# Gathers of the experts' results spread over 112 steps of attention instead of 32, with the division of the heads between them

## What is computed

```
xn = layernorm(x)
s = attention(xn)          # 4 batches x 16 heads of width 16, 2048 tokens
g = silu(experts(xn))      # 8 experts, the two best for each token
x = x + s * g
```

```
gathered = exp_out[flat_e, pos]
out = segment_sum(gates * gathered, tok)
```

## Time and profile before

| | us |
|---|---|
| median of 3 runs | 5480.47 (5478.05 to 5493.4) |
| the profiled execution | 5481.77 |
| its span in the trace | 5480.0 |

### The profile page before, as it was taken

The page is one execution under the profiler, slowest core; times in us unless marked ns, Lnnn a source line. Parts: engine busy times, 40 slices in busy tenths (PEclk is TensorE's granted clock), DMA queues, the critical chain, the costliest instruction groups (busy, mean ns, idle before and its releaser), DMA issues. The chain is left out here.

```text
span 5480.0 us, 91530 instructions
## 1 busy us (share of the span) xinstructions
PE 4872.8 (89%) x32641; PEld 2260.3 (41%) x32641; DVE 4207.0 (77%) x4885; ACT 3473.9 (63%) x6262; POOL 1685.5 (31%) x1155
## 2 busy tenths in 40 slices
PE   5767767768774999998999999999999999999998
PEld 3224224225222888887333333333333333333335
DVE  5997996997996223222888888999999999999996
ACT  5765765665662111111777778888888888888883
POOL 1864873882883222222333331100001000010003
PEclk8998998998996999999999999999999999999999
DMA  3304403003004655553222223211122111221116
GB/s 96 122 8 145 139 0 128 11 1 107 17 0 137 204 192 188 188 200 127 59 68 68 68 68 88 51 42 34 34 50 57 37 34 34 54 55 35 34 34 183
DMA packets 354710, 437.91 MB, mean 80 GB/s; under 512 B 172347, under 2 KB 305302, under 8 KB 343382
## 3 DMA queue, kind: packets, MB, share of 16 engines
q1 hardware_dynamic: 311142, 222.98, 14.7%
q0 software_dynamic: 42784, 208.59, 11.4%
q10 hardware_dynamic: 320, 0.39, 0.0%
HBM read 287.44 MB, written 145.96 MB: 79 GB/s over the span
## 5 line engine op out<-in xcount | busy, mean ns | idle before, releaser
L1603 DVE TENSOR_REDUCE at_mpart<-at_ps 128x1 f32<-128x1024 f32 x2048 | 2412.8, 1220 | 338.7 <-PE at_ps L1496 302.7
L1588 ACT ACTIVATE at_E<-at_ps 128x512 f32<-128x512 f32 x4096 | 2126.5, 599 | 520.1 <-PE at_ps L1508 495.7
L1508 PE MATMUL at_ps<-at_qs,at_ks 98*128 98x512 bf16 x4096 | 1246.6, 386 | 49.3 <-ACT at_E L1588 39.0
L1516 PE MATMUL at_ps<-at_E,at_vst 128*32 128x256 f32 x16400 | 1101.4, 386 | 1.3 <-issue 1.3
L1508 PEld LDWEIGHTS at_ps<-at_qs,at_ks 98*128 98x128 bf16 x4096 | 315.3, 97 | 867.7 <-ACT at_E L1588 651.7
L1494 PE MATMUL at_ps<-at_ks,at_qs 64*128 64x512 bf16 x2048 | 634.8, 385 | 7.0 <-DVE at_mpart L1603 3.9
L1496 PE MATMUL at_ps<-at_kb,at_qb 64*128 64x512 bf16 x2048 | 634.9, 385 | 0.0
L857 POOL TENSOR_TENSOR l_work<-l_work 128x1024 f32<-128x1024 f32 x256 | 604.8, 2363 | 78.5 <-DVE l_work L866 70.4
L1516 PEld LDWEIGHTS at_ps<-at_E,at_vst 128*32 128x32 f32 x16400 | 428.9, 109 | 412.2 <-ACT at_E L1588 196.3
L753 PE MATMUL l_ps<-l_bc,l_sel 96*128 96x512 bf16 x1024 | 313.3, 395 | 277.3 <-DVE l_work L866 126.8
L1312 ACT ACTIVATE at_late<-at_ps 128x256 f32<-128x256 f32 x288 | 110.6, 384 | 639.4 <-PE at_ps L1255 635.3
(11 more groups left out here) (246 smaller groups left out, 4641.3 us busy)
## 6 DMA issues: line engine op xcount, KB each, us to landing
at_ks<-kp SPq DMA_DIRECT2D x396, 64.0 KB
xd<-l_zero SPq DMA_DIRECT2D x4, 5120.0 KB, 33.6
yd<-l_zero SPq DMA_DIRECT2D x4, 5120.0 KB, 33.5
at_qs<-qp SPq DMA_DIRECT2D x132, 128.0 KB
at_qb<-qp SPq DMA_DIRECT2D x132, 128.0 KB
qp<-l_work SPq DMA_DIRECT2D x32, 384.0 KB
kp<-l_work SPq DMA_DIRECT2D x32, 384.0 KB
ot<-at_osb SPq DMA_DIRECT2D x516, 17.0 KB
```

Source lines behind the costliest of these rows:

```text
L1508: pe.matmul(S[chunk_bank(u, l)], m.ks[0:STACK + 2, j, bass.ts(kt, P)], m.qs[0:STACK + 2, j, half * QB + hf * BANK:half * QB + (hf + 1) * B ...
L1516: mm = pe.matmul(O[32 * q:32 * q + 32, :], m.vst[:, par, 2 * sl + kk, :], m.E[:, sl % 4, kk, bass.ts(q, QG)], start=(sl == 0 and kk == 0), ...
L1588: act.activation(m.E[:, sl % 4, c // 2, bass.ts(c % 2, BANK)], S[chunk_bank(u, l)], ACT.Exp, scale=SCALE).then_inc(s.ex, 1)
L1603: dve.tensor_reduce(m.mpart[:, job:job + 1], ring[n % 2].rearrange("p a b -> p (a b)"), AX_X, ALU.max).then_inc(s.ring_free, 1)
```

## The change

PACE goes from 2 to 7: the eight gathers of a group are released at offsets 0, 0, 1, 2, 3, 4, 5 and 6 steps instead of four and four in two steps, so that the sixteen groups take 112 steps. The division of a batch's heads, which stood behind all gathers, is cut in two functions, `load_heads` and `divide`, and called between groups: the loads behind groups 4, 9 and 13 (counted from 0), the rest behind groups 5, 10 and 14. The loads of `f0` and `x10` come last. What is computed is the same.

```diff
-def combine_experts(pool, io, m, s):
+def combine_experts(pool, io, m, s, load_heads, divide):
 
-    PACE = 2
+    PACE = 7
+    LOAD_BEHIND, DIVIDE_BEHIND = (4, 9, 13), (5, 10, 14)
...
             pool.dma_start(io.f[b:b + 1, :, part, :].rearrange("o p n -> (o p) n"),
                            m.fsum.rearrange("p i d -> p (i d)")).then_inc(m.moved, 16)
+            if done in LOAD_BEHIND:
+                load_heads(LOAD_BEHIND.index(done))
+            if done in DIVIDE_BEHIND:
+                divide(DIVIDE_BEHIND.index(done))
...
-            combine_experts(pool, io, m, s)
-            pool.dma_start(m.f0, io.f[0:1, :, :, :].rearrange("o p g (i d) -> (o p) (g i) d", d=D)).then_inc(m.early, 16)
-            pool.dma_start(m.x10, io.x1[0:1, :, :].rearrange("o (i p) d -> p (o i) d", p=P)).then_inc(m.early, 16)
-            done = 0
-            for b in range(B - 1):
+            def load_heads(b):
                 h0, stored = b * H1 + 1, H1 * (b + 1)
                 pool.wait_ge(o_st[0], 64 * (stored + 1) + OS0)
                 pool.wait_ge(o_st[1], 64 * stored + OS0)
...
+
+            def divide(b):
                 pool.wait_ge(m.recip, b + 1)
...
-                    done += 1
+                    done = 4 * b + q + 1
...
+            combine_experts(pool, io, m, s, load_heads, divide)
+            pool.dma_start(m.f0, io.f[0:1, :, :, :].rearrange("o p g (i d) -> (o p) (g i) d", d=D)).then_inc(m.early, 16)
+            pool.dma_start(m.x10, io.x1[0:1, :, :].rearrange("o (i p) d -> p (o i) d", p=P)).then_inc(m.early, 16)
             pool.wait_ge(m.early, 32)
```

## The result

| | us |
|---|---|
| the kernel before, 19 runs | 5485.38 (5467.6 to 5495.05) |
| the changed kernel, 19 runs | 5469.82 (5464.06 to 5484.58) |
| ratio | 0.998, 95% interval 0.997 to 0.9989 |
| span of the profiled execution | 5466.9 |

The change makes the kernel 0.2% faster. The interval leaves out 1, but the gain is less than the 0.3% from which the prediction would call it one. The forecast was 5466.6 and minus 0.25%. The number holds, and its sum doesn't: the trace shows that the steps of attention between the first and the last L1615 gave back nothing at all. A number that comes out of such a sum is luck.

The account below looks back on a forecast made before the run. Attention was taken as bound by a ring of PE, ACT and DVE hand-overs, where lateness is never caught up. -63.2 - 5 + 37.1 + 12.0 + 5.2 = -13.9 us gave 5466.6 us, minus 0.25%, range 5440 to 5492.

Parts of the forecast that it names:

- Removed, bursts of four: Attention's 30 steps with four gathers each: they cost 63.2 us more than plain steps, which the change removes.
- The first step: Attention's first step holds three gathers instead of eight: 5 us come back, between 2 and 8.
- Single gathers: 95 gathers with an attention step to themselves: 0.39 us each, 37.1 us added.
- Rival 1: A gather alone in an attention step is nearly free, at 0.1 us: 5428 us, chance 0.13.
- Rival 2: Dearness belongs to the step: a lone gather costs 1.2 us in some 55 odd steps: 5505 us, chance 0.13.
- Pairs: Fifteen groups begin with two gathers in one attention step: 0.80 us a pair, 12.0 us added.
- Dear steps: 13 places in 110 attention steps, eight steps apart, each give 0.4 us beyond a gather's usual price: 5.2 us added.
- Moved, the division: Batch loads and division between gather groups: DVE's wait for the sums isn't reached, margins 85 us and more: 0 us.
- beside the ring: POOL's products, sums and plain DMAs lie outside attention's PE, ACT and DVE hand-overs; steps kept their 21.2 us.
- The division's bursts: Three times `divide` holds up four or five gathers, which then come at once: 0 us, with 3 for the range.
- Moved, f0 and x10: These two loads come behind step 110, near 4980 us, with 390 us to spare before the output stage: 0 us.
- my rule: PE and ACT never wait, tensor_reduce doesn't contend with GpSimd, so gathers are free: sum 0, 5480 us, chance 0.05.

Follow-up runs that it names:

- before_again: The kernel before, unaltered, run for its trace on a chip of the experiments instead of the first chip: 5378.77 us.
- changed_again: The changed kernel, unaltered, on a chip of the experiments: 5422.88 us, ratio 1.0081 to the kernel before.
- both: Changed kernel with batch loads issued at an even step's start and each product waiting for the low row of maxima: 5381.84 us, ratio 1.0008 to the kernel before.

## Why the prediction was right in its number and wrong in its working

- **The number** was luck: 5466.6 for 5469.82, minus 0.25% for minus 0.2%. Gathers were priced at 54.3 us (37.1 + 12.0 + 5.2) and the trace has 13.0 in their steps, 41 too much. On the other side stand three costs put at nothing, 19.8 + 23.0 + 12.3 = 55.1 us. The other 13 are the first step (3.9 more than forecast), the rest of the kernel before's excess (64.4 + 3.8 for 63.2) and some 4 us outside attention's steps.
- **Removed, bursts of four, 63.2 us**: right on the chip it was read from; the changed trace has no such steps. (By plain steps of 21.09 and 21.23 it is 64.4; the 21.20 holds odd steps of 21.32.) It is not a price of the kernel: in `before_again` the same thirty steps hold 3.7 us, and on all three other chips the kernel takes some 100 us less.
- **The first step, 5 us**: it got shorter by 8.9. That the gathers did it was not tested on that chip; on another the first step takes 26.2 us with eight gathers (`before_again`) and 26.0 with three (`changed_again`).
- **Single gathers, 37.1 us: the failed step.** I took the first gather of a burst for a single one, since both start at +0.94. The 95 cost 0.1 us in 35 even steps and 8.0 in 42 odd ones (2.2 of it not theirs); the others share a step with something dearer. In even steps ACT's copy isn't late at all. In most odd steps, where SP issues loads beside the gather, it is late by the 0.47 us that I read, and only half or less of it reaches the step. What the burst's first gather pays in the even step of the earlier trace rows is thus a thing of bursts, or of what else is under way. Rival 1 had the price right, and I gave it 0.13; without the three costs put at nothing the span would have been 5466.9 - 55.1 = 5412 us (an estimate), beyond its 5428. Rival 2 had the place right, the odd steps, but at some 0.2 us a step and not 1.2.
- **Pairs, 12.0**: 4.9 in eleven steps. **Dear steps, 5.2**: none came eight steps apart.
- **Moved, the division, 0 us**: wrong. I asked only whether DVE would wait for the sums, and that margin held (L1636, the reciprocal, costs the same 1.3 us at each place). I didn't ask what the loads would be in front of. That POOL's plain DMAs "are beside the ring" was read off a stretch where the 2 MB start at a step's head; in mid-step behind a store they cost 23.0 us.
- **Products "beside the ring": wrong**, 19.8 us. In the kernel before each group ended in an odd step, its product behind the subtraction. With seven steps a group every second one ends in an even step, where POOL waits 1.9 us for the landing instead of 5 to 7, and the product begins at +3.8 instead of +7 to +9, before the subtraction at +5.24. In odd steps SP's loads are under way beside the gather; that it is they that slow its landing was not tested.
- **The division's bursts, 0 to 3 us**: 12.3 in nine steps on that chip, and 6.1 in the same steps of `changed_again`.
- **Moved, f0 and x10, 0 us**: right. From the last step's end to the end of the span it takes 97.3 us for 98.0.
- The Trainium skill's page SBUF — State Buffer, section "Who interferes with whom", says in the same list from which I took my rule that a DVE instruction with two SBUF inputs contends with a GpSimd instruction that reads SBUF. DVE's L1619 has two, and its 2.33 us for 0.27 beside POOL's product agrees. I had weighed the line that speaks for the reductions and not looked for DVE's other instructions. By the line that I did weigh (PE and ACT wait for nobody) the gathers would be free; the two later chips that were traced agree with that, and the earlier trace rows, where PE's results come late beside gathers, don't.
- **What stays open**: why gathers hold up PE's results on the first chip. There, before attention begins, the kernel is already 35 us later than in `before_again` (2588.6 and 2553.9), so attention is not the only place. The clock granted in the thirty steps is 0.99 there and 1.00 in `before_again`; plain steps take the same 21.09 us on both. None of the experiments ran on that chip, so neither the single gather's price nor the burst's was tried there by itself, and both edits' gains are measured on the others. For `both` there is only an estimate: 5466.9 - 19.8 - 23.0 = 5424 us of span there, 1% under the kernel before.

## What to carry to other kernels

When work is moved along a queue, list for each moved instruction what runs on the other engines at its new place, not only who waits for it: a DVE instruction of 0.27 us with two operands in SBUF cost 2 us a step under a POOL product, and 2.5 MB on POOL's queue, issued in mid-step in front of SP's small loads, cost 5 to 14 us. Tie such work to a semaphore that marks the place (here the low row for the product and the step's start for the loads); both edits together took 40 us off the changed kernel on one chip. Don't take the delay of one hand-over for the price of the step: 0.47 us late cost 0.23 and less. And a cost that is read in one trace on one chip (here 72 us of gathers) should be seen on a second chip before a kernel is arranged around it.

## What the runs showed of the hardware

- POOL's product of two SBUF operands holds DVE's instruction of two SBUF operands to its end: 0.27 us became 2.33 (3.40 in step 32 of `changed_again`, where the product began later), and 1.29 and 1.60 under the sum. DVE's 143 reductions from PSUM beside POOL's products and sums kept their 1.20 to 1.23 us.
- While POOL's queue had 1.38 MB to move, SP's got one packet in 12 us through on the same sixteen engines; with 0.62 MB it got 461.
- The same kernel took 5480 us on one chip and 5377 to 5384 on three others, with the same 21.09 us for a plain step. Between the two chips that have a trace of it, 67 us of the difference lie in attention, and 61 of them in the 30 steps in which POOL issued gathers.
